# Expert layers in a two-layer transformer kernel: eight of sixteen experts on their own tokens only

## The reference, cut to what matters

```python
# f1 and f2: a shared block of hidden size 1024, and 8 routed experts of hidden size 128, 2 per token
shared_out = silu(x @ sw1.T) * (x @ sw2.T) @ sw3.T
scores = sigmoid(x @ router_w.T)
_, top_idx = top_k(scores + expert_bias, 2)
top_scores = take(scores, top_idx); top_scores /= top_scores.sum() + 1e-9
routed_out = sum over the token's 2 experts of score * (silu(h1) * h2) @ w3[e]
# f3 and f4: 16 routed experts of hidden size 128, 2 per token
scores = softmax(x @ gate_w.T)
topk_w, topk_idx = top_k(scores, 2); topk_w /= topk_w.sum() + 1e-20
y = sum over the token's 2 experts of topk_w * (silu(x @ wg[e]) * (x @ wu[e])) @ wd[e]
```

## Time and profile before

| | |
|---|---|
| three timed runs | 2188.07, 2193.45, 2194.14 us; median 2193.45 |
| the profiled execution | 2188.24 us, its span 2186.5 us, 1.7 us around it |
| PE busy | 1921.2 us, 88% of the span |
| granted TensorE clock over the span | 0.924 of full |
| f1, from its first transfer to that of the next layer | 215.12 to 377.34, 162.2 us |
| f3, likewise | 795.63 to 966.06, 170.4 us |

### The profile page before, as it was taken

One profiled execution on the slowest core, in us unless ns is written; L12 is line 12 of the kernel. 1 busy time (PEld: TensorE's weight loads), 2 busy tenths in 40 slices (PEclk: granted clock), 3 DMA queues, 4 the chain that ended last, 5 costly groups with the idle time before them and its releaser, 6 DMA issues. The chain is left out here.

```text
span 2186.5 us, 33829 instructions
## 1 busy us (share of the span) xinstructions
PE 1921.2 (88%) x11802; PEld 1546.6 (71%) x11802; DVE 1344.4 (61%) x2478; ACT 935.1 (43%) x1643; POOL 702.7 (32%) x570
## 2 busy tenths in 40 slices
PE   6998898889846668985899999999999999997898
PEld 5334787678712247874788888888888888886687
DVE  4664544654469964455677766767667767664443
ACT  2454432333243223334455554545445455553332
POOL 3011333033377723324433322333223333220232
PEclk9899899889978879987899999999999999999899
DMA  3210122012100003320000000000000000000232
GB/s 80 48 30 8 53 75 80 24 45 84 57 0 0 0 15 112 117 80 3 8 6 11 8 12 11 11 4 11 12 11 12 11 9 11 8 6 15 94 103 79
DMA packets 44953, 74.60 MB, mean 34 GB/s; under 512 B 7360, under 2 KB 27456, under 8 KB 44800
## 3 DMA queue, kind: packets, MB, share of 16 engines
q1 hardware_dynamic: 44800, 72.56, 11.0%
HBM read 64.87 MB, written 1.25 MB: 30 GB/s over the span
## 5 line engine op out<-in xcount | busy, mean ns | idle before, releaser
L337 POOL TENSOR_TENSOR f_weighted<-f_hidden,f_comb_all 128x512 f32<-128x512 f32 x128 | 190.2, 1488 | 416.6 <-DVE f_hidden L400 344.6
L791 ACT ACTIVATE gqa_probs<-acc,gqa_bias,gqa_q_scale 128x128 f32<-128x128 f32 (+7 forms) x256 | 212.5, 830 | 259.1 <-DVE gqa_bias L882 258.8
L1050 PE MATMUL aux<-gqa_probsT,gqa_v 128*128 128x128 f32 x2304 | 308.5, 280 | 1.4 <-ACT gqa_oT L813 1.4
L878 DVE TENSOR_REDUCE gqa_neg_max<-acc 128x1 f32<-128x128 f32 (+7 forms) x256 | 193.6, 756 | 170.7 <-PE acc L1017 168.3
L1050 PEld LDWEIGHTS aux<-gqa_probsT,gqa_v 128*128 128x128 f32 x2304 | 285.5, 196 | 8.2 <-issue 5.1
L734 POOL TENSOR_TENSOR gqa_q_high<-gqa_straight,gqa_turned_q 128x512 fp32r<-128x512 f32 x64 | 81.5, 1273 | 504.9 <-DVE gqa_turned_q L839 504.9
L477 PE MATMUL aux<-xnT_high,f_w_high 128*128 128x512 f32 x512 | 212.5, 415 | 21.9 <-ACT f_silu_g L358 12.4
L400 DVE TENSOR_TENSOR f_hidden<-f_silu_g,aux 128x512 f32<-128x512 f32 x128 | 87.8, 686 | 228.5 <-ACT f_silu_g L358 124.1
L477 PE MATMUL aux<-xnT_low,f_w_high 128*128 128x512 f32 x512 | 209.7, 410 | 0.0
L477 PE MATMUL aux<-xnT_high,f_w_low 128*128 128x512 f32 x512 | 208.7, 408 | 0.0
L1034 PE MATMUL aux<-ident,gqa_probs 128*128 128x128 f32 x1152 | 180.8, 282 | 7.2 <-DVE gqa_probsT L910 4.6
(11 more groups left out here) (333 smaller groups left out, 4310.2 us busy)
## 6 DMA issues: line engine op xcount, KB each, us to landing
f_comb_all<-comb_by_expert SPq DMA_DIRECT2D x48, 512.0 KB, 3.9
f_w<-in_f_up SPq DMA_DIRECT2D x64, 256.0 KB, 3.5
f_w<-in_f_down SPq DMA_DIRECT2D x64, 128.0 KB, 3.7
mat_qk<-mat_high SPq DMA_DIRECT2D x64, 64.0 KB, 2.3
gqa_w_q<-in_g_wq SPq DMA_DIRECT2D x32, 128.0 KB, 2.1
gqa_wo<-in_g_wo SPq DMA_DIRECT2D x32, 128.0 KB, 2.1
mat_qk<-mat_low SPq DMA_DIRECT2D x32, 64.0 KB, 2.3
stream<-in_x SPq DMA_DIRECT2D x1, 1024.0 KB, 5.7
```

The lines of the kernel that those rows point to most:

```text
L337: pool.tensor_tensor(weighted[:, j % SLOTS], hidden[:, j % SLOTS], comb_all[:, j // 2 % 2, j % 2 * HALF:(j % 2 + 1) * HALF], ALU.mult).the ...
L791: act.activation(probs[:, j % 4, 0:width(j)], scores(j), ACT.Exp, bias=bias[:, j % 16:j % 16 + 1], scale=q_scale[:, j // NT % 2, tile_of(j ...
L878: dve.tensor_reduce(neg_max[:, j % 16:j % 16 + 1], scores(j), AX, ALU.max, negate=True).then_inc(max_ready, 1)
L1050: last = pe.matmul(aux[:, 2 + t // 4, t % 4 * P:(t % 4 + 1) * P], v[:, g, s, :], probsT[:, j % 4, s * P:(s + 1) * P], start=(s == 0), stop ...
```

## The change

Eight of the 16 experts (`DENSE`, those numbered 0 to 7) are computed on all tokens, as before. In f1 and f2 these are the shared block and need no weights; in f3 and f4 POOL still weighs them. The experts 8 to 15 are computed on their own tokens only:

1. DVE makes a 0/1 mask of token and expert. PE adds it up over tokens with nine matmuls of 8-column groups (`earlier`, `ones`), so each token learns how many tokens of its expert stand before it. DVE rounds the counts up to whole tiles of 128 and works out a slot for each of a token's two choices (`index`); choices of an expert under 8 go to rows behind the 23 tiles. It also finds which expert each of the 23 tiles has (`tile_expert`).
2. POOL issues 16 indirect transfers that scatter the normed rows (`xn`, 128 rows of 1 KB each) to `slots_dram`.
3. When all have landed, SP loads one tile of 128 slots after the other. For each tile PE turns it (`turn`), ACT and DVE split it (`part`), PE multiplies it by the weights of its expert (`rise`, which reads the expert's number into a register), ACT and DVE make the hidden values (`gate`); these are turned and split together with the tile three steps later, multiplied by the down weights, and copied to `y_tile`, which SP writes to `y_dram`.
4. When all 23 are written, POOL gathers with 16 indirect transfers two rows for each token, and DVE multiplies them by the token's shares and adds them to the stream, in 16 operations of 128x256.

Steps of all engines come from one list, `order()`: the head with the router, dense steps 1 to 9, the sparse stage of 27 steps (dense step 10 stands before its last), and dense steps 11 to 15. The layer is written out, with no hardware loop. At the end of the first attention layer SP clears both DRAM tensors with two transfers from the zero tile (2944 and 2048 rows of 1 KB).

```diff
+DENSE = 8
+FFN_TILES = 2 * NT + E - DENSE - 1
...
+        def sparse(s):
+            if s < TILES + 3:
+                steps.extend([("turn", s), ("part", s)])
+            if s == 0:
+                steps.append(("round", FRONT - 1))
+            if s < 2:
+                steps.append(("down", FRONT - 2 + s))
+            if s == 2:
+                steps.append(("split", 15))
+            if s >= 1:
+                steps.extend([("rise", s), ("gate", s)])
...
+            sp.wait_ge(scattered, 16 * 2 * NT)
+            for s in range(TILES + 5):
+                if s < TILES:
+                    if s >= 4:
+                        sp.wait_ge(xs_turned, s - 3)
+                    sp.dma_start(xs[:, s % 4, :], slots_dram[s * P:(s + 1) * P, :]).then_inc(tile_in[s % 4], 16)
+                if s >= 5:
+                    n = s - 5
+                    sp.wait_ge(y_ready, n + 1)
+                    sp.dma_start(y_dram[n * P:(n + 1) * P, :], y_tile[:, n % 3, :]).then_inc(y_stored[n % 3], 16)
...
-            pipeline(pool, 2 * E, [(0, weigh)], 8)
+            pool.wait_ge(index_ready, 2)
+            for t in range(NT):
+                for j in range(2):
+                    scatter(j, t)
+                if skip:
+                    weigh(t)
...
+            for r in range(3):
+                pool.wait_ge(y_stored[r], 16 * ((TILES - r + 2) // 3))
+            for t in range(NT):
+                for j in range(2):
+                    gather(j, t)
+                if skip and FRONT + 1 + t < 2 * DENSE:
+                    weigh(FRONT + 1 + t)
...
+                elif kind == "part":
+                    cols = part_cols(n)
+                    act.wait_ge(xs_turned, n + 1)
+                    if n >= 3:
+                        act.wait_ge(risen, n - 2)
+                    act.activation(part_high[:, n % 3, cols], aux[:, n % 2, cols], ACT.Copy).then_inc(part_high_ready, 1)
+                elif kind == "gate":
+                    act.wait_ge(risen, n)
+                    if n >= 4:
+                        m = n - 4
+                        if m >= 3:
+                            act.wait_ge(y_stored[m % 3], 16 * (m // 3))
+                        act.activation(y_tile[:, m % 3, :], aux[:, 2 + n % 2, D:2 * D], ACT.Copy).then_inc(y_ready, 1)
+                    if n - 1 < TILES:
+                        if n >= 3:
+                            act.wait_ge(s_hidden_ready, n - 2)
+                        act.activation(s_silu[:, n % 2, :], aux[:, 2 + n % 2, 0:P], ACT.Silu).then_inc(s_silu_ready, 1)
...
+            for j in range(2):
+                for t in range(NT):
+                    dve.wait_ge(gathered[t], 32)
+                    dve.wait_ge(added, 4 + t + 1 if j else t // 2 + 1)
+                    dve.scalar_tensor_tensor(core.x[:, t, :], y_back[j][:, t, :], share[:, j, t:t + 1], core.x[:, t, :],
+                                             ALU.mult, ALU.add).then_inc(added, 1)
...
+            def rise(s):
+
+                if s == 1:
+                    pe.wait_ge(hidden_ready, FRONT)
+                    pe.wait_ge(experts_ready, 1)
+                    pe.wait_ge(w_low_ready, last_sparse + 1)
+                elif s == 2:
+                    pe.wait_ge(silu_ready, FRONT)
+                else:
+                    pe.wait_ge(s_hidden_ready, min(s - 2, TILES))
+                if s >= 6:
+                    pe.wait_ge(y_ready, s - 5)
+                pe.wait_ge(part_low_ready, s)
+                r = (s - 1) % 3
+                if s - 1 < TILES:
+                    expert[s - 1] = pe.value_load(tile_expert[0:1, s - 1:s], min_val=0, max_val=DENSE - 1)
+                    for k in range(DC):
+                        rows = slice(k * P, (k + 1) * P)
+                        for m, (a, b) in enumerate(three(part_high[:, r, rows], part_low[:, r, rows],
+                                                         *sparse_weights(s - 1, slice(k * 2 * P, (k + 1) * 2 * P)))):
+                            last = pe.matmul(aux[:, 2 + s % 2, 0:D], a, b, start=k + m == 0, stop=(k, m) == (DC - 1, 2))
+                if s >= 4:
+                    for m, (a, b) in enumerate(three(part_high[:, r, D:], part_low[:, r, D:],
+                                                     *sparse_weights(s - 4, slice(UP, UP + D)))):
+                        last = pe.matmul(aux[:, 2 + s % 2, D:2 * D], a, b, start=m == 0, stop=m == 2)
+                last.then_inc(risen, 1)
...
+            nothing = core.zeros[:, :].bitcast(F32)
+            sp.dma_start(slots_dram[0:FFN_TILES * P, :].rearrange("(s p) d -> p s d", p=P),
+                         nothing.unsqueeze(1).to_broadcast([P, FFN_TILES, D])).then_inc(cleared, 16)
+            sp.dma_start(y_dram[FFN_TILES * P:, :].rearrange("(s p) d -> p s d", p=P),
+                         nothing.unsqueeze(1).to_broadcast([P, 2 * NT, D])).then_inc(cleared, 16)
+            sp.wait_ge(cleared, 32)
```

More of the change, by code:

```diff
@@ L299, in load_comb @@
[L299 to L319, removed]
+            def load(m):
+                e = LOADS[m]
+                if m >= STAGES:
+                    sp.wait_ge(w_low_ready, m - STAGES + 1)
+                sp.dma_start(w[:, m % STAGES, 0:UP], up_dram[e:e + 1].rearrange("a p k n -> (a p) (k n)")).then_inc(w_in[m % STAGES], 16)
+                sp.dma_start(w[:, m % STAGES, UP:], down_dram[e:e + 1].rearrange("a p n -> (a p) n")).then_inc(w_in[m % STAGES], 16)
@@ L321, in _ @@
+            if skip:
+                load_comb(7)
         @block.gpsimd
@@ L326, in _ @@
             norm.gpsimd(pool)
[L327 to L338, removed]
@@ L342, in _, with split @@
         @block.scalar
         def _(act):
[L344 to L349, removed]
+            def split(m):
+                e = LOADS[m]
+                act.wait_ge(w_in[m % STAGES], 32 * (m // STAGES) + 32)
+                if e >= DENSE:
+                    to = ws_high[:, e - DENSE, :]
+                else:
+                    if e >= SLOTS:
@@ L371, in _ @@
                 act.activation(probs[:, :, :], select[:, :, :], ACT.Exp).then_inc(exp_ready, 1)
[L372 to L381, removed]
@@ new lines, in _ @@
+            split(1)
+            hide(0)
+            many = [1, TILES, DENSE]
+            s.then(dve.tensor_tensor(passed[:], upto[0:1, :].unsqueeze(1).to_broadcast(many),
+                                     tile_start[:].unsqueeze(2).to_broadcast(many), ALU.is_le))
+            s.then(dve.tensor_reduce(tile_start[:], passed[:], AX, ALU.add))
+            dve.tensor_scalar(tile_expert[:], tile_start[:], DENSE - 1.0, None, ALU.min).then_inc(experts_ready, 1)
+            for j, best in enumerate((first, second)):
+                if j:
+                    dve.wait_ge(share_ready, 1)
+                dve.wait_ge(comb_ready, 1)
+                s.then(dve.tensor_tensor(pick[:], best[:, :, chosen], comb[:, :, chosen], ALU.mult))
+                dve.tensor_reduce(share[:, j, :], pick[:], AX, ALU.add).then_inc(share_ready, 1)
```

371 lines of the change are left out of this document (295 added, 76 removed).

## The result

| | before | after |
|---|---|---|
| median | 2192.35 us (4 runs) | 2234.92 us (4 runs, 2232.70 to 2241.81) |
| profiled execution, span | 2186.5 | 2230.9 |
| f1 / f2 | 162.2 / 161.7 | 174.3 / 177.9 |
| f3 / f4 | 170.4 / 169.4 | 185.0 / 185.4 |
| gqa | 1046.2 | 1031.6 |

The ratio is 1.0202 (1.0175 to 1.0230): 43 us slower, where 19 were forecast. The expert layers lost 58.9 us together, and gqa, in which nothing is changed, gained 14.6.

The account below looks back on a forecast made before the run. PE time was taken to bound the kernel. Per layer, -67.8 + 62.6 + 1.8 + 6.7 gave +3.3 us (f1, f2), +6.3 (f3, f4), together +19.2: median 2213 us, 0.9% slower, 8-in-10 range 2160 to 2290.

Parts of the forecast that it names:

- the 67.8 us removed: Expert layers: eight experts by two halves are 16 dense steps of 4.24 us no longer run, -67.8 us in each layer.
- sparse stage: The 23 expert tiles and draining steps, mostly at 2.7 us a step, add 62.6 us per layer.
- gathers beside the last dense steps: End of each expert layer: POOL's 16 gathers lie beside dense work and add 0 us.
- DVE's additions and the end: Behind the last down: DVE's 16 additions of 128x256 at 0.42 us add 6.7 us per layer, bounds 4 to 10.
- head: Layer start, with router and slots: +1.8 us in f1 and f2, 3 more in f3 and f4.
- 16 gathers ... Both hidden: In f1 and f2, 16 scatters (17.6 us) and 16 gathers (17.6 plus 2.1 landing) are covered by dense steps.
- Rival 2: Indirect transfers hold POOL 2.2 us each, delaying dense steps and layer ends: +94 us, 2306 us; chance 0.12.
- Rival 1: Sparse stage: register load in series and PE at the lower clock, 3.4 us a step, 2266 us; chance 0.20.
- rival 3: Sparse stage: tile loads land sooner, register load hidden, full clock, 2.07 us a step, 2165 us; chance 0.26.
- The head of f3 and f4: Start of f3 and f4: 1.8 us plus 3 for POOL's weighing behind two scatters and token weights going through DRAM.
- The chain in the sparse stage: ACT copy, SP store, next load, PE turn and multiply go round once in two steps; 2.7 us a step.
- The additions, the clearing and the gathers' issue on POOL: Layer end +6.7 us; SP's clearing before f1 adds nothing, 5 us at most; each POOL issue 1.1 us.

Follow-up runs that it names:

- e6: The changed kernel run again unaltered on the second chip: 2224.8 us, 1.0153 of the kernel before.
- e13: The changed kernel with the three edits, gathers back to back, on the fourth chip: 2139.3 us, 0.9773 of the kernel before.
- e1: The changed kernel with SP storing each finished tile two places later in its queue, first chip: 2149.5 us, 0.9818 of the kernel before.
- e9: The changed kernel a third time, unaltered, on the third chip: 2212.8 us, 1.0116 of the kernel before.
- e3: The changed kernel with POOL's 16 indirect gathers replaced by plain transfers of contiguous rows: 2205.6 us, 1.0088 of the kernel before.
- e4: The changed kernel with the 16 gathers left out, DVE adding what lies in the two tiles: 2202.3 us, 1.0071 of the kernel before.
- e8: The changed kernel with the three edits, on the second chip: 2136.3 us, 0.9742 of the kernel before.
- e2: The changed kernel with each step's expert number loaded into its register behind the previous step's matmuls: 2181.2 us, 0.9967 of the kernel before.
- e7: The changed kernel with both the later store and the early register load, second chip: 2155.4 us, 0.9841 of the kernel before.
- e10: The changed kernel with the later store again, on the third chip beside e9: 2149.0 us, 0.9813 of the kernel before.
- e15: As e13, with a POOL product behind each pair of gathers in f1 and f2, fourth chip: 2128.3 us, 0.9726 of the kernel before.
- the three edits: Changes to the changed kernel: later store, early register load, and in f3 and f4 SP issuing expert weights ahead of score loads; 2136.3 us on the second chip.
- e12: The changed kernel with the three edits and a POOL product behind each pair of gathers in f1 and f2, third chip: 2125.9 us, 0.9722 of before.
- e14: As e13, with plain transfers of contiguous rows in place of the indirect gathers, fourth chip: 2115.3 us, 0.9661 of the kernel before.

## Why the prediction was wrong

What each layer has in place of the 67.8 us removed, split by the prediction's terms. From the sparse stage the two `down` that stand in it are taken off; the tail is set against 26.4, the end against 2.5 us before; the rest is the head, from the layer's start to the first tile.

| us, to be set against the 67.8 removed | forecast | f1 | f2 | f3 | f4 |
|---|---|---|---|---|---|
| sparse stage | 62.6 | 60.3 | 61.0 | 61.1 | 61.6 |
| gathers beside the last dense steps | 0 | 9.7 | 10.0 | 1.5 | 3.8 |
| DVE's additions and the end | 6.7 | 6.7 | 6.5 | 8.7 | 8.1 |
| head | 1.8 (f3, f4 4.8) | 3.2 | 6.5 | 11.1 | 10.3 |

Against the forecast the layers have 25 us more by the gathers, 18 by the head, 3 by the end and 6 less by the sparse stage, 40 together; gqa, which no term covers, took 15 off.

**The step that failed is "16 gathers ... Both hidden".** In f1 and f2 the gathers did lie beside dense steps, and POOL was held 1.25 us for each, near the 1.1 taken. What was left out is that a row of them can hold ACT, DVE and PE up, which cost 20 us of the tails of f1 and f2 in the first profile and went with 5 more in f3 and f4; of the four chips used later two showed it (e6, e13) and two did not (e1, e9). Rival 2 named the right transfers and the wrong victim: POOL at 2.2 us a transfer was not seen, and its 94 us neither (of which its 14 for the gathers of f1 and f2 should read 12, 37 less 25). Rival 1 would need 3.4 us a step and rival 3 2.45 or less; both are out by the step measured. In f3 and f4 "hidden" failed in a second way: DVE's additions waited some 2 us for the last gathers in each (gone in e3 and e4).

**The head of f3 and f4 was sized too small:** 4.8 forecast, 11 and 10 measured, 9 and 11 in e9, where no engine had the waits. The prediction counted DVE's and POOL's work there and did not follow SP's queue, in which the weights stand behind `load_comb`. Moving the issues gave 7 to 8 us a layer back (e8), and then POOL's two scatters and a weighing took 4.4 us a step, not 3.7: the 16 scatters alone took 23 us in f1, 1.4 each. In f2, where 1.8 were forecast and 6.5 measured, two waits of ACT without a releaser, 3.3 and 2.6 us, stand beside the scatters (they end at 490.01 and 494.46 us).

**The chain in the sparse stage was right,** in its order and nearly in its sum: 2.70 to 2.83 us a step against 2.7. Three of its terms were off and cancelled in part: the store's issue 0.32 for 0.47, the turn 0.52 for 0.33, and the register load 0.3 a step for 0.12 (e2). The clock was 0.90 to 0.96, not 0.80; it is at 1.00 once the store has moved and PE no longer waits for tiles (e1, e7). The Trainium skill's floor of 600 ns for `tensor_load` (DMA: Bandwidth & Descriptors, "Latency and other measured facts") would have been the better value: the instruction is recorded with 0.30 us, and its removal shortened a round from 5.30 to 4.73.

**The additions, the clearing and the gathers' issue on POOL were right.** 16 additions took 6.4 us where nothing held them up (f1 and f2), and f1 began at 215.00 as before, 215.12.

**On a chip without the waits the forecast time is met, 2212.8 us for 2213, but not by its terms:** there the layers lost 40 us where 19 were forecast, and gqa gave 19 back, which no part of the prediction had. Sign and size then agree by two errors, which is luck.

## What to carry to other kernels

When a loop through DRAM sets the pace, look at the order of the issuing queue first: moving the store two places back in SP's queue was worth 64 us here (e9 to e10), while the whole change had cost 23 to 43. A register that addresses weights is loaded a step ahead, behind the matmuls. Indirect transfers of POOL beside busy engines are better spread out than issued in a row where the chip shows the waits (11 us less, e13 to e15); where it does not, the spacing costs 4.6 us at the end of f1 and of f2. A difference of 1% between two kernels wants both on one chip.

With the three edits the changed kernel beats the one before by 2.3 to 2.6% (e8, e13), and with spaced gathers by 2.7 to 2.8% whether the chip shows the waits or not (e12, e15).

## What the runs showed of the hardware

- Indirect transfers in a row (16, of 128 rows of 1 KB, 1.25 us apart) went with waits of up to 14.5 us on ACT (some 3 of them are its usual pause), and shorter ones on DVE and PE, on some chips and none on others. The packets of the gathers in f1 took the same median of 159 ns on both, so the transfers were not slower themselves. POOL differs too: in f1 and f2 three of the 16 gathers are recorded with 1.4 us and not 0.95 where there are no waits (e1, e2, e9, e10), and one at most where there are. What holds the engines up was not found.
- A register load of one number from SBUF on PE is recorded with 0.30 us. Between two dependent groups of matmuls it made a round of the chain 0.57 us longer (5.30 against 4.73, e2).
- Indirect gathers of 128 KB landed 2.7 to 2.8 us after their issue (e9), plain transfers of POOL of the same size 2.3 to 2.4 (e3, e14), plain loads of SP 2.1 to 2.2 (medians).
